# Moving the additions that finish the rotated keys from POOL to DVE in a fused token-mixing, attention and feed-forward kernel

## The reference

```
h = tok(x)                           # 16 tokens -> 8: q,k,v by small matrices, softmax over 8, out = q + attn @ v
h = h + attn(layernorm(h))           # 12 query heads, 3 key/value heads of 64, rotary q and k, softmax, @ Wo
h = h + ffn(layernorm(h))            # 192 -> 768, gelu, 768 -> 192

def apply_rope(x, cos, sin):
    x1, x2 = x[..., :d], x[..., d:]
    return concatenate([x1 * c + x2 * s, -x1 * s + x2 * c], axis=-1)
q = apply_rope(q, cos, sin); k = apply_rope(k, cos, sin)
scores = einsum('bhqd,bhkd->bhqk', q, k) * SCALE
```

## Time and profile before

| | us |
|---|---|
| median of 3 runs | 1139.42 |
| lowest and highest | 1138.35 and 1139.71 |
| the profiled execution, its own time | 1139.55 |
| its span on the core | 1137.7 |

### The profile page before, as it was taken

The page is one execution under the profiler, slowest core; times in us unless marked ns, Lnnn a source line. Parts: engine busy times, 40 slices in busy tenths (PEclk is TensorE's granted clock), DMA queues, the critical chain, the costliest instruction groups (busy, mean ns, idle before and its releaser), DMA issues. The chain is left out here.

```text
span 1137.7 us, 24489 instructions
## 1 busy us (share of the span) xinstructions
PE 1021.7 (90%) x7232; PEld 870.5 (77%) x7232; DVE 795.0 (70%) x1967; ACT 725.3 (64%) x2530; POOL 485.9 (43%) x711
## 2 busy tenths in 40 slices
PE   3788999999999999999999999999999999999986
PEld 2567878887877887787888787787778788878765
DVE  2566777777777776777777777777677777777751
ACT  2455666676676677666667667667766666766752
POOL 0434544444544453444444454445344444445440
PEclk7799999999999999999999999999999999999999
DMA  5223434343433433443433343343334343334231
GB/s 161 68 81 113 134 98 122 107 115 105 136 114 102 126 103 115 120 133 97 123 106 115 107 136 113 104 126 103 113 122 132 95 125 105 114 108 136 94 111 46
DMA packets 139935, 127.49 MB, mean 112 GB/s; under 512 B 30992, under 2 KB 123024, under 8 KB 139920
## 3 DMA queue, kind: packets, MB, share of 16 engines
q1 hardware_dynamic: 137632, 124.16, 36.8%
q10 hardware_dynamic: 2288, 3.15, 0.8%
HBM read 70.63 MB, written 56.62 MB: 112 GB/s over the span
## 5 line engine op out<-in xcount | busy, mean ns | idle before, releaser
L408 POOL TENSOR_TENSOR E<-E,e_rcp 128x512 f32<-128x512 f32 x192 | 199.6, 1040 | 401.6 <-DVE e_rcp L528 401.6
L298 ACT ACTIVATE E<-ring,m_neg 128x128 f32<-128x128 f32 x768 | 270.8, 396 | 104.6 <-DVE m_neg L510 104.6
L298 ACT ACTIVATION_READ_ACCUMULATOR E<-ring,m_neg 128x1 f32 x768 | 181.2, 236 | 0.0
L392 POOL TENSOR_TENSOR q_tok<-rot_c,rot_s 128x384 f32<-128x384 f32 x128 | 125.2, 999 | 129.4 <-DVE rot_s L499 129.4
L510 DVE TENSOR_REDUCE m_neg<-ring 128x4 f32<-128x512 f32 x192 | 120.7, 684 | 81.5 <-PE ring L694 81.5
L811 PE MATMUL ring<-wo_sb,OT 128*128 128x192 f32 x768 | 140.0, 333 | 9.4 <-ACT OT L306 9.4
L520 DVE STREAM_TRANSPOSE EB<-E 128x512 f32<-128x512 f32 x192 | 133.7, 696 | 20.3 <-POOL E L408 20.3
L681 PE MATMUL bank<-wout_sb,G 128*128 128x192 f32 x768 | 135.4, 326 | 2.7 <-ACT G L364 2.7
L811 PEld LDWEIGHTS ring<-wo_sb,OT 128*128 128x128 f32 x768 | 124.5, 192 | 16.4 <-ACT OT L306 16.4
L293 ACT COPY qkT<-ring 128x512 f32<-128x512 f32 x128 | 69.4, 593 | 92.8 <-PE ring L673 92.8
L681 PEld LDWEIGHTS bank<-wout_sb,G 128*128 128x128 f32 x768 | 125.4, 190 | 3.3 <-ACT G L364 3.2
(11 more groups left out here) (122 smaller groups left out, 2352.6 us busy)
## 6 DMA issues: line engine op xcount, KB each, us to landing
spill<-EB SPq DMA_DIRECT2D x64, 512.0 KB, 2.6
ET<-spill SPq DMA_DIRECT2D x256, 128.0 KB, 2.8
spill<-EB SPq DMA_DIRECT2D x64, 256.0 KB, 2.0
ET<-spill SPq DMA_DIRECT2D x256, 64.0 KB, 2.3
x_sb<-in_x_dram SPq DMA_DIRECT2D x64, 192.0 KB, 2.5
out_dram<-out_sb SPq DMA_DIRECT2D x64, 96.0 KB, 2.3
x_sb<-in_x_dram SPq DMA_DIRECT2D x64, 64.0 KB, 2.3
w_raw<-in_w_att_dram ACTq DMA_DIRECT2D x2, 576.0 KB, 4.8
```

The source lines that it names most:

```text
L298: last = nc.scalar.activation(E[:, a, s * P:(s + 1) * P], RING[a][:, s * P:(s + 1) * P], ACT.Exp, bias=m_neg[:, a, s:s + 1], accum_out=e_s ...
L392: nc.gpsimd.tensor_tensor(q_tok[:, a, c], rot_c[:, a, c], rot_s[:, a, c], ALU.add).then_inc(q_out, 1)
L408: nc.gpsimd.tensor_tensor(e, e, r, ALU.mult).then_inc(prob_out, 1)
```

## The change

The two additions for the keys leave POOL's `turned_in` and become `keys_added` on DVE, with a semaphore `k_out` of their own that is counted once for both. DVE does them right behind `rotate(a)`: for a = 0 ahead of the copy of the values, for a = 1 ahead of `normalise(h2, ..., 1)`. They wait for DVE's own `rot_out` (the products must have been written) and for `qT_mm` of the pair before (PE must have read the old `k_tok`). POOL adds the queries alone, and `q_out` counts to 2 for each sequence where it counted to 4. PE waits on `k_out` ahead of block 6.

```
                 def turned_in(a):
+                    need(pool, qT_mm, 4 * (p - 1) + 2 * a + 2)
+                    for b in range(2):
                         pool.wait_ge(rot_out, 6 * p + 3 * a + b + 1)
-                        if b < 2:
-                            ... (queries)
-                        else:
-                            c = slice(DQ, DQ + 2 * HD)
-                            nc.gpsimd.tensor_tensor(k_tok[:, a, 0:2 * HD], rot_c[:, a, c], rot_s[:, a, c],
-                                                    ALU.add).then_inc(q_out, 1)
-                            ...
-                            nc.gpsimd.tensor_tensor(k_tok[:, a, 2 * HD:].rearrange("p (o d) -> p o d", o=2),
-                                                    kc, ks, ALU.add).then_inc(q_out, 1)
+                        c = slice(b * BANKW, (b + 1) * BANKW)
+                        nc.gpsimd.tensor_tensor(q_tok[:, a, c], rot_c[:, a, c], rot_s[:, a, c],
+                                                ALU.add).then_inc(q_out, 1)
...
                 def rotate(a, banks):
-                        need(dve, q_out, 8 * (p - 1) + 4 * a + 4)
+                        need(dve, q_out, 4 * (p - 1) + 2 * a + 2)
...
+                def keys_added(a):
+                    need(dve, qT_mm, 4 * (p - 1) + 2 * a + 2)
+                    dve.wait_ge(rot_out, 6 * p + 3 * a + 3)
+                    c = slice(DQ, DQ + 2 * HD)
+                    nc.vector.tensor_tensor(k_tok[:, a, 0:2 * HD], rot_c[:, a, c], rot_s[:, a, c], ALU.add)
+                    c = slice(DQ + 2 * HD, DQ + DKV)
+                    kc, ks = (r[:, a, c].rearrange("p (o d) -> p o d", o=1).broadcast_to([P, 2, HD]) for r in (rot_c, rot_s))
+                    nc.vector.tensor_tensor(k_tok[:, a, 2 * HD:].rearrange("p (o d) -> p o d", o=2),
+                                            kc, ks, ALU.add).then_inc(k_out, 1)
...
                     rotate(0, (0, 1, 2))
+                    keys_added(0)
                     v_out_of_psum(0)
...
                     rotate(1, (0, 1, 2))
+                    keys_added(1)
                 if ffn:
                     dve.wait_ge(ln2_rs, 2 * p)
                     normalise(h2, mv2, rs2, hn, 1).then_inc(hn_out, 1)
...
                 def qk_turned(a):
-                        if t in (0, 3, 6):
-                            pe.wait_ge(q_out, 8 * p + 4 * a + (1, 2, 4)[t // 3])
+                        if t in (0, 3):
+                            pe.wait_ge(q_out, 4 * p + 2 * a + t // 3 + 1)
+                        if t == 6:
+                            pe.wait_ge(k_out, 2 * p + a + 1)
```

More of the change, by code:

```diff
@@ L167, in program @@
         rot_out = sem("rot_out")
-        v_out, q_out = sem("v_out"), sem("q_out")
+        v_out, q_out, k_out = sem("v_out"), sem("q_out"), sem("k_out")
         qT_mm, qT_out = sem("qT_mm"), sem("qT_out")
@@ L383, in rstd2, with turned_in @@
                                             ALU.pow).then_inc(ln2_rs, 1)
[L385 to L388, removed]
+                def turned_in(a):
+                    need(pool, qT_mm, 4 * (p - 1) + 2 * a + 2)
+                    for b in range(2):
                         pool.wait_ge(rot_out, 6 * p + 3 * a + b + 1)
-                        if b < 2:
-                            c = slice(b * BANKW, (b + 1) * BANKW)
-                            nc.gpsimd.tensor_tensor(q_tok[:, a, c], rot_c[:, a, c], rot_s[:, a, c],
-                                                    ALU.add).then_inc(q_out, 1)
-                        else:
-                            c = slice(DQ, DQ + 2 * HD)
-                            nc.gpsimd.tensor_tensor(k_tok[:, a, 0:2 * HD], rot_c[:, a, c], rot_s[:, a, c],
[L397 to L400, removed]
-                            nc.gpsimd.tensor_tensor(k_tok[:, a, 2 * HD:].rearrange("p (o d) -> p o d", o=2),
-                                                    kc, ks, ALU.add).then_inc(q_out, 1)
+                        c = slice(b * BANKW, (b + 1) * BANKW)
+                        nc.gpsimd.tensor_tensor(q_tok[:, a, c], rot_c[:, a, c], rot_s[:, a, c],
+                                                ALU.add).then_inc(q_out, 1)
                 def probs(a, g, q):
@@ L410, in step @@
                 if att:
-                    turned_in(0, (0, 1, 2))
+                    turned_in(0)
                 if ffn:
@@ L419, in step @@
                 if att:
-                    turned_in(1, (0, 1, 2))
+                    turned_in(1)
                     wait_apart(pool, pool_passed, (h2_out, 2 * p))
```

## The result

| | before | changed |
|---|---|---|
| median, us | 1139.57 (1138.35 to 1140.29) | 1155.83 (1154.68 to 1157.32) |
| ratio to the kernel before | | 1.0145 (95%: 1.0127 to 1.0162) |
| the profiled execution, us | 1139.55 | 1155.92 |
| its span, us | 1137.7 | 1154.0 |

The forecast was 1161, within 1148 to 1167. Both profiled executions lie near their medians, so the traces can be compared: 16.3 us more of span.

What follows compares the result with a forecast made beforehand. PE's program, with PE busy 90% of the span, was taken to bound the kernel. 31 x 0.73 = 22.6 us, less 1.0 in step 0, gave +21.6 on 1139.55, so 1161 us, range 1148 to 1167.

Steps and rivals of the forecast that it cites:

- The bound: In the loop, PE's program sets the time, 31.39 of 33.60 us busy; its wait at L801 for `hn` matters.
- 31 x 0.73: `hn` of the second sequence comes 0.73 us later in steps 1 to 31, 22.6 us in all.
- A two-input addition blocks and is blocked: DVE's additions with two SBUF inputs take turns with POOL's instructions, as in step 0: 1.17 against 0.45 us.
- Steps 1 to 5 of the sum: Second half of a step: first addition, POOL's copy, second addition, `hn`, then PE's L801, in turn, +0.73 us.
- First half: nothing: First half of a step: more than 2 us of DVE's idle time hides the two additions, no cost.
- PE has as many waits as before: PE's waits stay equal in number, as do those of DVE's rotation; no term in the sum.
- Step 0: -1.0 us: In step 0 PE waits for the keys, and DVE's additions come ahead of L465: -1.0 us.
- Passed on in full: Everything PE does behind L801 waits behind it, so the late end of `hn` goes into the step in full.
- Both rivals without a block: In the loop the new additions run unblocked: level, around 1139.5 us, chance 0.08; with a gain, around 1135, chance 0.06.
- the second: No block, and POOL's copy does not hold L479 as L396 did: -0.11 x 31 - 1.0 = -4.4 us, 1135, chance 0.06.
- Partly taken up: Later `hn` shortens PE's next wait, L730, leaving half the price: +10 us, around 1149, chance 0.08.

Runs made afterwards that it cites:

- experiment 1: Changed kernel with the second input of both key additions read from PSUM instead of SBUF, keys wrong: 1134.61 us, ratio 0.9955.
- experiment 2: Changed kernel with POOL's copy of `h_cur` waiting for `hn` of the second sequence: 1145.87 us, ratio 1.0051.
- experiment 5: Changed kernel with the key additions of the second sequence given back to POOL, DVE adding only those of the first: 1136.39 us, ratio 0.9957.
- experiment 4: Kernel before with PE's two waits ahead of the scores swapped, values first, transposed queries and keys second: 1135.97 us, ratio 0.9966.
- experiment 6: Kernel before with, ahead of the loop: weight subtractions later, 1141.88 us; 24 PE transposes, 1137.47; step 0 second-sequence keys on DVE, 1137.96; first three keys on DVE, 1136.59.
- experiment 7: Changed kernel, second-sequence keys behind `hn`: POOL's copy waiting for `hn`, 1131.60 us; second query addition waiting too, 1122.83; kernel before with only the query wait, 1141.81.

## Why the prediction was right

Point by point, by its own steps.

1. *The bound.* PE's waits decided, and L801 was the place. Right: 22.2 us more wait there, while the forecast of 31 x 0.73 said 22.6. One row was misread: of the 0.9 us that PE waits for `k_tok`, the second place (0.28 us, at 74.64) lies in step 1, not in step 0.
2. *A two-input addition blocks and is blocked.* Right, and shown by experiment 1: with one SBUF input the same additions take 0.29 us, with two they take 0.85.
3. *Steps 1 to 5 of the sum.* First addition 0.15 us behind POOL's queries (forecast 0.15); the copy next (shown by experiment 2); second addition 0.14 us behind it (0.15); `hn` free at 0.37 and 0.30; PE +0.71 us (0.73).
4. *First half: nothing.* Right (experiment 5).
5. *"PE has as many waits as before".* True of the waits, but this step took the instructions between them for nothing. A register instruction went away behind the wait that ends last, and gave back 0.07 us in a step (experiment 4), about 2 us in all. The order of PE's instructions at `scores` would have shown it, and had not been compared.
6. *Step 0: -1.0 us.* The term was mis-sized. The lead was 4.0 us in the traces. The collision of L401 was counted, PE's clock was not, though the windows of the trace before show half the clock in 52 to 58 us. How the 4.0 us divide between the two stays open (experiment 6).
7. *Passed on in full.* Right: L733 still waits 0.94 us. From step 1 to step 31 the start of `hn` of the first sequence goes from 4.0 us early to 15.1 us late (1084.36 against 1099.41), 0.64 us in each of 30 steps. With the last steps, 1.2 us, that makes the 16.3 us of the span.

The forecast of 1161 was 5 us too high, by about 2 us of point 5 and 3 us of point 6, and the direction and the mechanism held. The price of the block itself, 0.73 against 0.71 us, was right by its own steps and not by errors that cancel: both errors went the same way. Both rivals without a block fell in experiment 1. The kernel in which the additions do not meet POOL took 1134.6 us, where they said 1139.5 and 1135; the second comes this close by the lead ahead of the loop, not by the shorter step that it named. "Partly taken up" fell with point 7.

## What to carry to other kernels

Before work is moved from POOL to DVE, look at what POOL does at that moment. In this kernel an addition on DVE with two SBUF inputs, or the one-input layer norm in SBUF, ended only 0.12 to 0.16 us behind POOL's current instruction if POOL was already under way. The profile shows no wait for it, only a longer instruction (0.85 us in place of 0.28, 1.01 in place of 0.38). Put the result that the busiest engine waits for first, and the rest behind it. And a wait that keeps the other engine out of the way can be worth more than the work that it delays (1122.8 us in experiment 7).

## What the runs showed of the hardware that I had not expected

- The turns are exact to some hundredths: in the changed kernel the first of the two additions, 128 columns, ended 0.14 to 0.16 us behind POOL's queries all 64 times, whether it was 0.32 or 0.96 us long. The Trainium skill (SBUF — State Buffer, "Who interferes with whom") describes this block as one of whole instructions. The trace agrees, and shows besides that POOL's copy lost only 0.07 us by it (0.57 against 0.50), although DVE's addition ran for the first 0.21 us of it: it ended 0.36 us behind that addition.
- A register instruction on PE between two waits costs 0.07 us if the earlier wait ends last (experiment 4), and nothing that shows if the order is turned. It has no row in the trace.
- With PE kept busy through one gap of step 0 the granted clock stayed at 1.00 in 52 to 58 us and was 0.50 in 64 to 68 us (experiment 6). `hn` of step 1 came only 0.5 us earlier.
